# Graph attention layer on one core: the loop over pairs of groups written as one turn per pair, on VectorE, TensorE and the DMA queue

## What is computed

```python
# layer 1: an MLP over every edge, gated, averaged per node of src
h = tanh(concat(x[src], x[dst]) @ W0 + b0); h = tanh(h @ W1 + b1)
h = (h @ W2 + b2) * (edge_attr @ Wg)
x = layernorm(x + segment_mean(h, src))
# layer 2: attention with 4 heads of 64
h = einsum('ni,hio->hno', x, W)
e = leaky_relu(attn_src[:, src] + attn_dst[:, dst], 0.2) * edge_weight
e_exp = exp(e - max(e))
out = segment_sum(h[:, src] * e_exp / denom[dst], dst)     # denom = segment_sum(e_exp, dst)
x = layernorm(x + out)
```

## Time and profile before

| | |
|---|---|
| median of 3 runs | 2240.55 us (2239.36 to 2241.13) |
| span of the profiled execution, first to last instruction | 2239.4 us; the lowest run is 2239.36, so next to nothing lies around the span |
| mean granted TensorE clock | 0.924 of 2.4 GHz |
| busy over the whole span | PE 1938.9, DVE 1513.0, POOL 1488.4, ACT 1377.2 us |
| the stage of the change | from the first gather of Hg, 1672.5 us, to the last `hist`, 2185.7 us |

### The profile page before, as it was taken

How to read it: one execution, slowest core, us unless ns; L and a number is a source line. 1 busy time by engine, 2 the same in 40 slices (tenths; PEclk the granted TensorE clock), 3 DMA queues, 4 the chain that set the end, 5 groups by cost and what they waited for, 6 DMA issues and landing times.

```text
span 2239.4 us, 40504 instructions
## 1 busy us (share of the span) xinstructions
PE 1938.9 (87%) x12932; PEld 1717.4 (77%) x12932; DVE 1513.0 (68%) x3765; ACT 1377.2 (62%) x2758; POOL 1488.4 (66%) x1229
## 2 busy tenths in 40 slices
PE   7799999999999999999999999999664676666660
PEld 6699999999999999999999999999653455445450
DVE  6566676676666766766666667666565766666667
ACT  3488888888888888888888888888550000000012
POOL 0427677777777677777776767775427777777754
PEclk9899999999999999999999999999886767877785
DMA  7988877777777777776777777776555566656544
GB/s 241 297 221 188 201 167 171 165 161 172 158 168 171 149 167 159 154 167 152 159 165 149 166 159 154 167 153 129 119 183 142 148 160 158 161 154 162 155 125 128
DMA packets 233059, 370.78 MB, mean 166 GB/s; under 512 B 32743, under 2 KB 165825, under 8 KB 232839
## 3 DMA queue, kind: packets, MB, share of 16 engines
q0 software_dynamic: 101232, 188.20, 42.2%
q1 hardware_dynamic: 131607, 179.89, 27.5%
HBM read 270.57 MB, written 97.40 MB: 164 GB/s over the span
## 4 chain that ended last, share of the span: by engine, by line
PE 70%; POOL 14%; DMA 6%; issue 5%; DVE 4%; ACT 1%; SPq 0%; DVEq 0%; ACTq 0%; POOLq 0%
PE bank L1483 16%; PE bank L1482 16%; PE bank L1484 16%; POOL Hg L1407 13%; PE bank L1536 5%; PE bank L1527 5%; PE bank L1553 3%; DMA Hg<-HT,src_c 3%; PE bank L1577 2%; PE bank L1578 2%; PE bank L1589 2%; PE bank L1588 2%; DMA accA<-ystage,to_a 1%; PE bank L1654 1%; DVE xb L959 1%
## 5 line engine op out<-in xcount | busy, mean ns | idle before, releaser
L1369 POOL DMA_INDIRECT accA<-ystage,to_a x391 | 653.6, 1672 | 244.0 <-DMA accA<-ystage,to_a 113.9
L1375 POOL DMA_INDIRECT GA<-TA,src_c x391 | 424.9, 1087 | 292.7 <-issue 95.4
L1407 POOL DMA_INDIRECT Hg<-HT,src_c x391 | 378.3, 968 | 121.1 <-issue 112.8
L1482 PE MATMUL bank<-h1h,W1h 128*128 128x512 f32 x882 | 348.4, 395 | 0.0
L1484 PE MATMUL bank<-h1h,W1l 128*128 128x512 f32 x882 | 347.5, 394 | 0.0
L1483 PE MATMUL bank<-h1l,W1h 128*128 128x512 f32 x882 | 347.5, 394 | 0.0
L563 DVE TENSOR_TENSOR h2l<-h2f,h2h 128x512 fp32r<-128x512 f32 (+1 forms) x294 | 203.1, 691 | 200.8 <-ACT h2l L1769 130.5
L1698 PE MATMUL bank<-xb,in_window 128*128 128x260 f32 (+1 forms) x782 | 273.1, 509 | 58.6 <-issue 56.9
L1944 ACT ACTIVATE drop<-neg_m 128x1 f32<-128x1 f32 x49 | 14.4, 295 | 455.0 <-DVE neg_m L954 455.0
L563 DVE TENSOR_TENSOR h1l<-h1f,h1h 128x512 fp32r<-128x512 f32 x294 | 195.1, 691 | 129.5 <-ACT h1h L1769 129.5
L1698 PEld LDWEIGHTS bank<-xb,in_window 128*128 128x128 f32 (+1 forms) x782 | 190.4, 256 | 103.9 <-issue 68.4
(11 more groups left out here) (217 smaller groups left out, 4819.2 us busy)
## 6 DMA issues: line engine op xcount, KB each, us to landing
TW<-TB SPq DMA_DIRECT2D x196, 203.0 KB, 3.5
ef<-in_eT SPq DMA_DIRECT2D x97, 256.0 KB, 4.6
bcast_i<-in_src_row SPq DMA_DIRECT2D x97, 256.0 KB, 5.6
HB<-hist SPq DMA_DIRECT2D x98, 130.0 KB, 3.1
rel<-RL SPq DMA_DIRECT2D x97, 128.0 KB, 5.6
rem<-RD SPq DMA_DIRECT2D x48, 256.0 KB, 4.6
TB<-stB SPq DMA_DIRECT2D x24, 406.0 KB, 4.5
accA<-zeros SPq DMA_DIRECT2D x4, 1677.0 KB, 13.7
```

The costliest lines, as they stand in the source:

```text
L1369: return pool.indirect_dma_start(out=table, out_offset=bass.IndirectOffsetOnAxis(ap=rows, axis=0), in_=sums, in_offset=None, compute_op=AL ...
L1375: pool.indirect_dma_start(out=GA[0:n, b % (GAR * BLOCKS_PER_GROUP), :].bitcast(f32), out_offset=None, in_=TA, in_offset=bass.IndirectOffse ...
L1407: pool.indirect_dma_start(out=Hg[0:n, slot, :], out_offset=None, in_=HT, in_offset=bass.IndirectOffsetOnAxis(ap=src_c[0:n, b:b + 1], axis= ...
L1482: pe.matmul(o, lh, rh, start=first, stop=False)
```

## The change

DVE: two one-hots and one window matrix stand ahead of the loop. A turn q is then: scores of q, one-hot of q+2, maximum of q, carries of 2q-2 and 2q-1, window matrix of q+1, weighting of 2q and of 2q+1, and the rare extra steps. PE: spread of q, destination scores of q+1, sums of 2q and of 2q+1. The DMA queue loads remainders 4 ahead and stores the two groups of the turn before. No instruction of the stage is added or removed.

```diff
             window_scores(0)
-            for q in range(-3, NQ + 1):
-                if 0 <= q < NQ:
-                    weighted_rows(2 * q)
-                if 0 <= q - 1:
-                    carry_window(2 * q - 2)
-                if 0 <= q + 1 < NQ:
-                    running_maximum(q + 1)
-
-                if 0 <= q + 2 < NQ:
-                    edge_scores(q + 2)
-                if 0 <= q < NQ:
-                    weighted_rows(2 * q + 1)
-                if 0 <= q - 1:
-                    carry_window(2 * q - 1)
-                if q + 3 < NQ:
-                    one_hot(q + 3)
-                if 0 <= q + 1 < NQ:
+            one_hot(0)
+            one_hot(1)
+            window_rows(0)
+            for q in range(NQ):
+                edge_scores(q)
+                if q + 2 < NQ:
+                    one_hot(q + 2)
+                running_maximum(q)
+                for g in (2 * q - 2, 2 * q - 1):
+                    if g >= 0:
+                        carry_window(g)
+                if q + 1 < NQ:
                     window_rows(q + 1)
-                if q >= 0 and 2 * q % ADC == 2 and 2 * q // ADC + 1 < NG // ADC:
+                weighted_rows(2 * q)
+                weighted_rows(2 * q + 1)
+                if 2 * q % ADC == 2 and 2 * q // ADC + 1 < NG // ADC:
                     window_scores(2 * q // ADC + 1)
                 if q == ADC // 4:
                     last_rows()
+            carry_window(NG - 2)
+            carry_window(NG - 1)
...
-            for q in range(-5, NQ):
-                if q + 5 < NQ:
-                    load_remainders(q + 5)
-                if q >= 0:
-                    for g in (2 * q, 2 * q + 1):
+            for q in range(-4, NQ + 1):
+                if q + 4 < NQ:
+                    load_remainders(q + 4)
+                if q >= 1:
+                    for g in (2 * q - 2, 2 * q - 1):
                         sp.wait_ge(s_carry, g + 1)
...
-            for q in range(-3, NQ):
-                if q >= 0:
-                    window_sums(2 * q)
-                if 0 <= q + 2 < NQ:
-                    spread_maxima(q + 2)
-                if q >= 0:
-                    window_sums(2 * q + 1)
-                if q + 3 < NQ:
-                    destination_scores(q + 3)
+            destination_scores(0)
+            for q in range(NQ):
+                spread_maxima(q)
+                if q + 1 < NQ:
+                    destination_scores(q + 1)
+                window_sums(2 * q)
+                window_sums(2 * q + 1)
```

## The result

| | before | after |
|---|---|---|
| median of 17 runs each | 2241.13 us | 2245.76 us (2243.41 to 2253.38) |
| ratio | | 1.0025, 95% interval 1.0018 to 1.0031 |
| span of the profiled execution | 2239.4 us | 2247.4 us (its own time 2249.02) |
| last `hist` | 2185.19 | 2193.57 us |
| first gather of the stage | 1672.5 | 1672.3 us |

The changed kernel is slower by 0.25%, some 5 us. The forecast was 2247.5. One correction to what stands above: some 1.6 us lie around a profiled span (2249.02 against 2247.4), so the span of before was likely not that of its lowest run. It changes no difference.

What follows compares the result with a forecast made beforehand. POOL's gathers bound the kernel before; a 10.06 us ring through TensorE was to set the pace after. 2173.2 + 2.2 + 5.8 + 6.2 + 4.7 put last `hist` at 2192.1, 6.9 us later: 2247.5 us, range 2238 to 2268.

Steps and rivals of the forecast that it cites:

- the ring through TensorE: Each turn, spread waits behind both sums, then maximum, weighting and next sums wait in turn: 10.06 us, equal to eight gathers.
- The 4.66 us from spread to sums: From start of the spread to first window sum of the same pair, through maximum, carries, window matrix and weighting: 4.66 us.
- The sums, 5.40 us: A pair's 16 window sums on TensorE, back to back, at the stage's average clock: 5.40 us per turn.
- The first pair at 7.60 us: First pair's window sums fall into the low clock: 7.60 us instead of 5.40, adding 2.2 us.
- `last_rows`, 5.8 us: One `last_rows` of 8.97 us on VectorE, not covered by TensorE's sums, adds 5.8 us.
- `window_scores`, 1.03 each: Six `window_scores` of 4.24 us on VectorE add 1.03 us each, 6.2 in all.
- The mean ring: Average turn from spread to spread: 48 at 10.06 us (482.9), plus 2.2, 5.8 and 6.2 for first pair and rare steps.
- Signs in the profile: `top_g` waits 2 to 4 us a turn, gather waits fall to tens, L1687 repeats every 10.1 to 10.3 us.
- The drain's gain of 5.2 us: Last scores to last `hist`, with one pair left to weight: 8.3 us instead of 13.47, if nothing else holds the turn.
- The first rival: Clock stays high in the 16 sums (3.79 us), gathers keep the pace, drain gain is won: 2233.5 us; chance 0.13.
- The third rival: Longer turn: 16 sums take 6.26 us, giving 10.73 us a turn and 2280 us; chance of more than 2264: 0.11.
- The gathers' meetings with L897: VectorE's L897 may slow gathers: up to 13 us lost; result within 0.2%, chance 0.10 with other mixtures.

Runs made afterwards that it cites:

- number 3: Changed kernel plus 12 useless TensorE products ahead of each pair's window sums, to hold the clock up; 2230.56 us, ratio 0.9962.
- number 4: Changed kernel with `last_rows` moved from turn 3 to ahead of the loop; 2242.73 us, ratio 1.0011.
- number 12: Changed kernel run again, unaltered, on chip C; 2246.16 us, ratio 1.0019.
- 1: Changed kernel with the next pair's spread placed between the two window sums on TensorE; 2232.43 us, ratio 0.9965.
- 2: Changed kernel with each pair's own window matrix built in its turn, ahead of the maximum; 2235.21 us, ratio 0.9978.
- 9: Changed kernel with both carries moved behind the two weightings, on chip C; 2234.41 us, ratio 0.9968.
- 11: Changed kernel with own window matrix ahead of the maximum, carries behind the weightings, `last_rows` ahead of the loop, chip C; 2235.46 us, ratio 0.9968.
- number 6: Kernel before with the spread behind both window sums on TensorE, on chip B; 2405.3 us, ratio 1.0033.

## Why the prediction was right

It said slower, 2247.5 us in a range of 2238 to 2268, by the ring through TensorE; measured 2245.76. By its steps:

- **The 4.66 us from spread to sums**: 4.66 in the turn shown, but by two errors that cancel. `top_g` follows the start of the spread after 0.42 us, not 0.53 (the spread takes 0.39 where TensorE comes straight from the sums, 0.49 where it stood); the second carry follows after 0.62 us, not 0.52, inside the bounds given (0.52 to 0.69) but not at the value taken.
- **The sums, 5.40 us**: 5.27 or 5.9. In the turns without rare steps the round was 10.16 on average against 10.06. This was the term that the sign hung on, and number 3 shows it: at 3.75 us the same order is some 14 us faster.
- **The first pair at 7.60 us**: it took 5.9 (the spread's second start is 10.68 us behind the first). The granted clock was 0.50 up to some 1694.9 us, 4.7 us into the sums, and 1.00 behind that; I had priced all 16 at 0.50. 1.7 us too much. Why it rose there is not shown.
- **`last_rows`, 5.8 us**: 15.55 against 10.06, so 5.5; its move took 3.5 us off the stage (number 4) and some 3 off the median, the rest being work that came in ahead of the loop.
- **`window_scores`, 1.03 each**: turns of 11.0 us between 9.93 and 10.55 ones, 0.4 to 1.1.
- **The mean ring** was 10.38; the forecast's sum gives (482.9 + 2.2 + 5.8 + 6.2) / 48 = 10.36. From the first sum of pair 0 to the first of the last pair the forecast has 497.1 us and the trace 497.1 (1690.20 to 2187.32). That it agrees so well is luck: 40 ordinary turns took 4 us more than forecast, and the first pair, the rare steps and the last turn, which builds no window matrix (3.53 us from spread to sums, not 4.66), 4 us less. The last `hist` was put at 2192.1 and came at 2193.57, in number 12's execution at 2190.19. The last sums took 6.21 us in the one and 3.31 in the other, against 4.7.
- **Signs in the profile**: the wait ahead of L1686 down from 142.6 to 21.0 us, `top_g` waiting 2.8 us a turn (2 to 4 said), L921 down to 7 us (a few tens said), last scores 10 us behind the last landing if that took the usual 3 us (8 to 12 said), from there to the last `hist` some 24 us (over 20 said). One sign did not come as said: the spread was to repeat every 10.1 to 10.3 us. The mean is near that, but hardly a turn is; most take 9.93 or 10.55.
- **The drain's gain of 5.2 us** was real but bought nothing in the changed kernel. It is cashed in number 3, where from last scores to last `hist` 8.39 us pass (8.3 said, at the high clock), and in numbers 1 and 2, 8.75 and 8.78.
- **The first rival** (clock high, gathers keep the pace, 2233.5) had the right place and price: number 3 makes that clock and gives 2230.56, numbers 1, 2, 9 and 11 reach it by a shorter ring, 2232 to 2235. It lost because the clock did not stay up by itself: 0.77 in 1772 to 2172 us before and after. The third rival, a longer ring, describes the turns of 10.55 us, but these were a minority.
- **The gathers' meetings with L897**: the gathers took 5.9 us over their median before, 2.5 of it one gather beside `last_rows` and not L897; now a gather takes 962 ns on average instead of 968 (the longest 3446 ns, now 2399). Nothing was lost there, little won.

The spread never started ahead of the sums queued before it: in 41 of 48 turns it starts 0.22 us behind the start of the last sum, in the others later. By the rule of the Trainium skill (TensorE: Matmul & The Clock Gate, Step-by-step: what each phase is for), that matmuls stay in program order, the spread could not overtake the sums; the trace agrees: only its weight loads run ahead. In the turn shown they start at 2091.75, 0.22 us ahead of the spread.

## What to carry to other kernels

Before taking a software pipeline's lead out of a loop, walk once round every cycle that the queues then close (here VectorE, TensorE, VectorE) and add up one round; compare it with the pace of whatever bounds the loop, not with each engine's busy share. A round equal to the pace is already a loss, since no rare delay is ever worked off. And if the shorter drain is wanted, put on the slack side of the cycle what does not belong in it: the spread between the sums, or the carries behind the weighting, turned 0.25% slower into some 0.3% faster on chips A and C. On chip B, where gathers land late, the kernel with the carries moved was 1.4% slower than before; so the reckoning is shown only where gathers land in some 3 us.

## What was not expected of the hardware

- Useless products made the program faster: 24 passes of 128 columns in each pause of TensorE brought the granted clock of 1772 to 2172 us from 0.77 to 0.94 and 16 sums from 5.43 to 3.75 us.
- The ring's length was not spread out but mostly took two values, 9.93 and some 10.55 us, in both profiled executions of the changed kernel, and with them the two lengths of the sums. In the turn below, after TensorE stood 3.7 us, the clock falls from 2.4 to 1.2 GHz some 0.7 us after the sums begin (2086.70) and is back before they end; in both profiled executions the two lengths held for hundreds of microseconds. The turn (us; PE, PEld, DVE, ACT, POOL busy; granted clock; DMA share; GB/s):

```profile
2086.00:2087.00 1.00, 0.30 (x2) 0.30 (x3) 1.00 (x2) 0.00 (x0) 0.69 (x2) 1.00 0.59 156
2087.00:2088.00 1.00, 1.00 (x5) 0.81 (x4) 0.96 (x3) 0.00 (x0) 0.69 (x2) 0.69 0.40 99
2088.00:2089.00 1.00, 1.00 (x4) 0.80 (x3) 0.90 (x5) 0.00 (x0) 0.69 (x2) 0.50 0.53 133
2089.00:2090.00 1.00, 1.00 (x3) 0.77 (x3) 0.22 (x1) 0.00 (x0) 1.00 (x1) 0.50 0.48 133
2090.00:2091.00 1.00, 1.00 (x4) 0.79 (x3) 0.00 (x0) 0.00 (x0) 0.69 (x2) 0.60 0.62 152
2091.00:2092.00 1.00, 1.00 (x7) 0.85 (x6) 0.00 (x0) 0.00 (x0) 0.69 (x2) 1.00 0.86 165
```

- The kernel before took 2240 us on chips A and C and 2397 on B. In number 6 a gather took POOL 0.957 us there (median), about as elsewhere (0.953), but landed tens of microseconds later.
